# A gated cross-attention block with routed experts: final loads released by a counted quota, a shared unit moved ahead of the expert loop, half of the last additions moved to GpSimd

## What is computed

```python
x = x + tanh(g_xattn) * attention(layernorm(x), ctx, ctx, mask, Wq, Wk, Wv, Wo, 16)
h = layernorm(x)
shared = (silu(h @ Sg.T) * (h @ Su.T)) @ Sd.T
probs = sigmoid(h @ router.T + bias); scores, idx = top_k(probs, 2); scores /= scores.sum(-1)
combined = sum over the two experts e of score_e * ((silu(h @ G[e]) * (h @ U[e])) @ D[e])
x = x + tanh(g_ffn) * (shared + combined)
```

## Time and profile before

| | us |
|---|---|
| median of three timed runs | 181.72 |
| lowest, highest | 181.02, 184.23 |
| the profiled execution's own time | 181.07 |
| its span, first to last instruction | 179.3 |
| busy in the span: TensorE, DVE, ACT, GpSimd | 165.0, 126.9, 109.3, 108.4 |

### The profile page before, as it was taken

One profiled execution on the slowest core, in us unless ns is written; L12 is line 12 of the kernel. 1 busy time (PEld: TensorE's weight loads), 2 busy tenths in 40 slices (PEclk: granted clock), 3 DMA queues, 4 the chain that ended last, 5 costly groups with the idle time before them and its releaser, 6 DMA issues.

```text
span 179.3 us, 4668 instructions
## 1 busy us (share of the span) xinstructions
PE 165.0 (92%) x1424; PEld 140.2 (78%) x1424; DVE 126.9 (71%) x613; ACT 109.3 (61%) x402; POOL 108.4 (60%) x137
## 2 busy tenths in 40 slices
PE   7899889999999999999999999988899999998960
PEld 7777669988889998779998779876586887886840
DVE  2779988756898766798776798778746666663364
ACT  3657997468588267598367698513546666663210
POOL 3666799846796816866706868686444666666200
PEclk9999999999999999999999999999999999999997
DMA  5999994900000000101000000013132222211063
GB/s 154 262 372 375 412 410 191 385 23 4 16 0 18 0 2 4 32 19 44 1 4 0 15 21 32 15 49 91 45 89 65 63 66 78 73 53 35 12 223 117
DMA packets 11095, 17.34 MB, mean 97 GB/s; under 512 B 2075, under 2 KB 6945, under 8 KB 10944
## 3 DMA queue, kind: packets, MB, share of 16 engines
q1 hardware_dynamic: 9504, 14.59, 24.0%
q0 software_dynamic: 1280, 2.20, 3.7%
q10 hardware_dynamic: 288, 0.26, 0.4%
HBM read 9.99 MB, written 7.51 MB: 98 GB/s over the span
## 4 chain that ended last, share of the span: by engine, by line
PE 62%; DVE 13%; ACT 8%; DMA 6%; POOL 5%; issue 4%; SPq 1%
PE misc L397 8%; PE pt L650 7%; PE s_even L360 6%; PE o_bank L386 6%; ACT probs L716 4%; PE pt L371 4%; PE proj_q L317 3%; DMA wq_raw<-wqT 3%; PE proj_k L317 3%; DVE probs L925 3%; PE proj_k L319 2%; PE pt L641 2%; PE proj_k L318 2%; PE proj_q L319 2%; PE proj_q L318 2%
## 5 line engine op out<-in xcount | busy, mean ns | idle before, releaser
L716 ACT ACTIVATE probs<-probs,negmax 128x128 f32<-128x128 f32 x128 | 50.0, 395 | 8.5 <-DVE negmax L925 8.5
L1311 POOL TENSOR_TENSOR probs<-probs,rinv 128x512 f32<-128x512 f32 x32 | 33.1, 1046 | 24.6 <-DVE rinv L939 24.3
L1420 POOL DMA_INDIRECT ys<-probsT,xg x23 | 22.5, 979 | 17.2 <-issue 10.7
L716 ACT ACTIVATION_READ_ACCUMULATOR probs<-probs,negmax 128x1 f32 x128 | 24.4, 191 | 0.0
L925 DVE CUSTOM_DVE_ANT_0 probs<-s_even,mask 128x128 f32<-128x128 f32 x64 | 18.1, 282 | 3.8 <-issue 3.8
L1341 POOL DMA_INDIRECT xs<-xrow,slot x16 | 16.3, 1019 | 6.5 <-issue 3.9
L371 PE MATMUL pt<-ident_sb,probs 128*128 128x128 f32 x128 | 17.6, 277 | 1.6 <-POOL probs L1311 1.1
L360 PE MATMUL s_odd<-kT,qT 64*128 64x128 f32 x128 | 18.5, 285 | 0.0
L360 PE MATMUL s_even<-kT,qT 64*128 64x128 f32 x128 | 18.5, 284 | 0.0
L925 DVE CUSTOM_DVE_ANT_0 probs<-s_odd,mask 128x128 f32<-128x128 f32 x64 | 18.1, 283 | 0.0
L650 PEld LDWEIGHTS pt<-down_sb,v 128*128 128x128 f32 x92 | 12.1, 190 | 7.2 <-issue 7.1
(11 more groups left out here) (279 smaller groups left out, 455.0 us busy)
## 6 DMA issues: line engine op xcount, KB each, us to landing
xs<-pad SPq DMA_DIRECT2D x5, 858.0 KB, 5.8
xg<-xs SPq DMA_DIRECT2D x23, 66.0 KB, 1.9
down_sb<-down SPq DMA_DIRECT2D x1, 1152.0 KB, 8.9
probs<-ys SPq DMA_DIRECT2D x4, 256.0 KB, 4.0
gu_raw<-gu SPq DMA_DIRECT2D x3, 256.0 KB, 6.5
wk_raw<-wkT SPq DMA_DIRECT2D x2, 256.0 KB, 3.8
wq_raw<-wqT SPq DMA_DIRECT2D x2, 256.0 KB, 5.0
mask<-mask SPq DMA_DIRECT2D x8, 64.0 KB, 2.0
```

The costliest lines, as they stand in the source:

```text
L716: e = act.activation(probs[:, r, l, :], probs[:, r, l, :], ACT.Exp, bias=negmax[:, r, l:l + 1], scale=-1.0, accum_out=rowsum[:, r, l:l + 1])
L1311: pool.tensor_tensor(quad, quad, rinv[:, r, 4 * u:4 * u + 4].unsqueeze(2).to_broadcast([P, 4, P]), ALU.mult).then_inc(norm_done, 1)
L1420: pool.indirect_dma_start(out=ys, out_offset=bass.IndirectOffsetOnAxis(ap=xg[n % IN_FLIGHT][:, P:P + 1].bitcast(U32), axis=0), in_=y_sb[n ...
```

## The change

- `FEWEST` = 2 is the least number of blocks with rows on any `y_out` semaphore. DVE's new `quota_steps`, at the end of round 10, make eight integers in two small dependent instructions: 32 or 48, according to whether block 16 + i holds rows.
- SP loads these eight into registers behind its last gather, waits on each `y_out` for the register's value, issues the four loads and its two stores, and only then waits for all 23 scatters.
- Shared unit 0 takes the place of `stay_warm(6)` ahead of the loop, unit 1 takes the place in round 3, and the order behind the loop is pass 2 (with the last block's down inside), pass 3, `down_step(0)`, `down_step(1)`. The silu of unit 0 moves to round 0 on ACT, its product to round 1 on DVE.
- For this the router of the sequences 6 and 7 moves from the banks `proj_q` and `proj_k` to `pt0` and `pt1`, and `down_step(0)` from `pt0` to `proj_k`.
- GpSimd, behind its last scatter, adds the first expert's rows to all four chunks. DVE adds the second expert's, and the shared expert last, after each pair of chunks. The stores wait for that.

```diff
-        shared_banks = [(proj_bank["q"], proj_bank["k"]), (o_bank, misc), (s_bank[0], s_bank[1]), (proj_bank["q"], proj_bank["k"])]
-        d_bank = [pt_bank[0], proj_bank["q"]]
+        shared_banks = [(proj_bank["q"], proj_bank["k"]), (proj_bank["q"], proj_bank["k"]), (o_bank, misc), (s_bank[0], s_bank[1])]
+        d_bank = [proj_bank["k"], proj_bank["q"]]
...
-        route_bank = [misc, misc, proj_bank["q"], proj_bank["q"], proj_bank["k"]]
+        route_bank = [misc, misc, proj_bank["q"], pt_bank[0], pt_bank[1]]
...
-            engine.wait_ge(sum_ready, n + 1)
+            engine.wait_ge(acc_done, 1 + n // 2)
...
+            def quota(i):
+                return sp.value_load(quotas[0:1, i:i + 1], min_val=16 * FEWEST, max_val=16 * (FEWEST + 1))
+
+            sp.wait_ge(quota_ready, 2)
+            due = [quota(i) for i in range(IN_FLIGHT)]
             for i in range(IN_FLIGHT):
-                sp.wait_ge(y_out[i], 16 * len(range(i, BLOCKS, IN_FLIGHT)))
+                sp.wait_ge(y_out[i], due[i])
             for n in range(4):
                 load_y(sp, n)
             store_out(sp, 0)
             store_out(sp, 2)
+            for i in range(IN_FLIGHT):
+                sp.wait_ge(y_out[i], 16 * len(range(i, BLOCKS, IN_FLIGHT)))
...
-            stay_warm(6)
+            pe.wait_ge(counts_read, 1)
+            shared_pass(0, 0)
+            shared_pass(0, 1)
...
                 if n + 2 == EARLY:
-                    pe.wait_ge(counts_read, 2)
-                    shared_pass(0, 0)
-                    shared_pass(0, 1)
+                    pe.wait_ge(h_done, 1)
+                    shared_pass(1, 0)
+                    shared_pass(1, 1)
...
-            shared_pass(1, 0)
+            shared_pass(2, 0)
             block_down(BLOCKS - 1, experts[BLOCKS - 1])
-            shared_pass(1, 1)
-            pe.wait_ge(h_done, 1)
-            shared_pass(2, 0)
             shared_pass(2, 1)
-            down_step(0)
+            pe.wait_ge(hid_ready, BLOCKS)
             shared_pass(3, 0)
             shared_pass(3, 1)
+            down_step(0)
             down_step(1)
...
+            def quota_steps():
+
+                beyond = float(IN_FLIGHT * FEWEST - EARLY) + 0.5
+                dve.tensor_scalar(more[:], iota_sb, beyond, upto[:, CANDIDATES - 1:], ALU.add, ALU.is_le).then_inc(quota_ready, 1)
+                dve.wait_ge(quota_ready, 1)
+                dve.tensor_scalar(quotas[:], more[:], 16.0, 16.0 * FEWEST, ALU.mult, ALU.add).then_inc(quota_ready, 1)
...
+                if n == 1:
+                    hidden(0)
...
+                if n == 2 * EARLY:
+                    quota_steps()
...
-            add_shared(0)
...
+            for half in range(2):
+                for n in (2 * half, 2 * half + 1):
+                    tiles = slice(2 * n, 2 * n + 2)
+                    dve.wait_ge(first_added, n + 1)
+                    dve.tensor_tensor(x_sb[:, tiles, :], y_of[:, tiles, 1, :], x_sb[:, tiles, :], ALU.add).then_inc(second_added, 1)
+                dve.wait_ge(second_added, 2 * half + 2)
+                add_shared(half)
...
+            for n in range(4):
+                tiles = slice(2 * n, 2 * n + 2)
+                pool.wait_ge(in_y[n], 16)
+                pool.tensor_tensor(x_sb[:, tiles, :], y_of[:, tiles, 0, :], x_sb[:, tiles, :], ALU.add).then_inc(first_added, 1)
```

More of the change, by code:

```diff
@@ L40 @@
 IN_FLIGHT = 8
+FEWEST = TOKENS * TOP_K // P // IN_FLIGHT
 EPS = 1e-5
@@ L127, in build @@
         slot = sb("slot", [P, B, TOP_K], U32)
+        more, quotas = sb("more", [P, IN_FLIGHT]), sb("quotas", [P, IN_FLIGHT], I32)
         total, share = sb("total", [P, B]), sb("share", [P, B])
@@ L204, in build @@
         at_ready, counts_read = sem("at_ready"), sem("counts_read")
+        quota_ready = sem("quota_ready")
         table_step, table_ready = sem("table_step"), sem("table_ready")
@@ L209, in build @@
         th_done, hidT_ready, yb_done, y_ready = sem("th_done"), sem("hidT_ready"), sem("yb_done"), sem("y_ready")
-        first_added, sum_ready = sem("first_added"), sem("sum_ready")
+        first_added, second_added = sem("first_added"), sem("second_added")
         xs = nc.dram_tensor("xs", (SLOTS, WIDTH), F32).ap()
@@ L215, in build @@
         y_rows = probs.rearrange("p r l k -> p (r l) k")[:, 0:B * TOP_K, :]
+        y_of = y_rows.rearrange("p (b k) h -> p b k h", k=TOP_K)
         def load_y(engine, n):
@@ L416, in x2_transposes @@
                 if r == LAST:
-                    pe.wait_ge(k_free, PROJ_USES * PAIRS)
+                    pe.wait_ge(pt1_free, GROUPS)
+                elif r == 3:
+                    pe.wait_ge(pt0_free, GROUPS)
                 elif r:
                     pe.wait_ge(at_ready, r)
-                if r == 3:
-                    pe.wait_ge(counts_read, 1)
                 for i, b in enumerate(ROUTED[r]):
@@ L863, in _ @@
                     block_y(n - 1)
+                if n == 0:
+                    silu(0)
                 if n + 2 == EARLY:
-                    silu(0)
+                    silu(1)
             block_y(BLOCKS - 1)
-            for unit in range(1, 4):
+            for unit in range(2, 4):
                 silu(unit)
@@ L1258, in _ @@
                 if n + 1 == EARLY:
-                    hidden(0)
+                    hidden(1)
+                if n == 2 * EARLY:
+                    quota_steps()
             block_hidT(BLOCKS - 1)
-            for unit in range(1, 4):
+            for unit in range(2, 4):
                 hidden(unit)
-            add_shared(0)
[L1264 to L1273, removed]
+            for half in range(2):
[5 more added lines that the diff above has]
+                add_shared(half)
         @block.gpsimd
```

## The result

The changed kernel takes 180.72 us in the median of 20 executions (178.97 to 181.66), the kernel before 181.25 of 20; the ratio is 0.9958 with a 95% interval of 0.9938 to 0.9978. It is faster, by some 0.8 us where 2.2 were forecast, and lies 0.02 above the upper end of the range given (177.6 to 180.7). The profiled execution took 181.44 us with a span of 179.4, itself 0.7 above the median. Medians are of executions at the usual granted clock; one of e12, 187.09 us at a clock of 0.855, is left out.

The account below looks back on a forecast made before the run. TensorE's chain and the result rows' landing were taken to end nearly together, the rows becoming the bound; 2.3 us saved at the additions less 0.15 for stores gave 178.9 us (179.0 for a median), range 177.6 to 180.7.

Parts of the forecast that it names:

- TensorE's tail: Behind the loop: six matmuls (1.4 us) and the 1.41 us idle gap go; down_step(1) ends at 171.25, 3.2 us earlier.
- Ahead of the loop: Six passes of unit 0 replace stay_warm(6) and end at 121.03: cost 0, bounds 0 to 0.3; silu and product 0, at most 0.6.
- The quota steps: Two dependent small DVE steps in a loop round, hidden by nothing: 0.3 us once, bounds 0 and 0.5.
- First load issued 166.16: SP waits for blocks 0 to 20 alone, 3.05 us sooner: first load at 165.86 plus 0.3, landed 169.76.
- The additions: Behind the first landing at 169.8, GpSimd's and DVE's additions with both add_shared end at 174.8 against 177.12: 2.3 us saved.
- The mutual hold-up: GpSimd's and DVE's adds wait for each other except the last 0.18 us; a round of both takes 0.97.
- the rule to the letter: Holder keeps the shared pair for its whole instruction: a GpSimd and DVE round takes 1.15, the sum 0.36 us more.
- The stores: At the end the last two stores go together, not 0.8 apart: 0.15 us taken, at most 0.33.
- the third (loads not early): SP's count still includes the last blocks, so the loads go no earlier: 182.0 us; chance 0.04.
- The fourth (start of the loop): Pass, silu and product of unit 0 hit the loop's start, up to 0.6 + 0.3 on top: 179.8 us; chance 0.09.
- The first: GpSimd and DVE do not hold each other up in the final additions, 0.85 less: 178.1 us; chance 0.20.
- The second: GpSimd takes each next chunk before DVE gets in, so DVE starves, 1.0 more: 180.0 us; chance 0.17 with its kin.

Follow-up runs that it names:

- e12: e10 with down_step(0) in round 22, ahead of the last but one block's down: 178.59 us, ratio to the kernel before 0.9868.
- e4: Changed kernel with only the moved units, banks and new order; waits for all scatters, additions in the old order on DVE: 181.22 us, ratio 0.9997.
- e3: Changed kernel without quota_steps and registers, the counts written as constants for this input (21 blocks), loads still early: 180.04 us, ratio 0.9921.
- e1: Changed kernel with all eight additions on DVE, shared expert still last, GpSimd adding nothing: 180.69 us, ratio 0.9952.
- e5: Changed kernel, but DVE begins its additions only when GpSimd has done all four: 181.91 us, ratio 1.0042.
- e9: Changed kernel with quota_steps in round 3, where DVE idles beside the shared unit, instead of round 10: 179.87 us, ratio 0.9940.
- e10: e9 with all additions on DVE in the earlier order: add_shared(0), chunks 0 and 1, add_shared(1), chunks 2 and 3: 178.72 us, ratio 0.9867.
- e11: e10 with 16 instead of 8 buffers for gathered rows and results, seven registers read: 178.51 us, ratio 0.9846.
- e8: The kernel before with only the early loads, counts as constants for this input (21 blocks): 180.99 us, ratio 0.9997.
- e2: Changed kernel without quota_steps and register waits; SP waits for all 23 scatters by constants: 182.16 us, ratio 1.0047.
- e6: Changed kernel with quota_steps in round 21 instead of round 10: 181.18 us, ratio 1.0012.

## Why the prediction was wrong

- **TensorE's tail: right.** The gap of 1.41 us is gone and the two down_steps follow each other, behind a loop that ended 1.36 late: 172.5 against 171.25 + 1.36 = 172.6. The result rows became the bound, as forecast.
- **Ahead of the loop: right.** The six passes (119.85 to 121.47) end where stay_warm ended, and DVE had no wait for unit 0's product; e4 shows the loop's length unchanged within 0.2 us.
- **The quota steps: mechanism right, size too small.** Forecast 0.3; the profile shows 0.45 at the steps, and e3 says 0.7 for the whole kernel. In the same three profiles (the changed kernel, e1, e5) the scatter of the block just behind the steps took 3.3, 3.7 and 3.2 us to land; in the changed kernel the chain shows what that costs. Whether the steps cause that was not isolated; one of 3.0 stands there in the kernel before too.
- **"First load issued 166.16": the step that failed.** It came at 167.98, 1.82 late. 1.05 of it is the scatter of block 20 starting at 164.94, against 163.59 + 0.3. Of this, 0.61 was lost ahead of the loop's first scatter, 0.45 of it in a stretch that did not change; the rest is the quota steps' excess of 0.15 and the gather that waited for a scatter. Another 0.65 is that scatter's own landing, 2.76 us where its counterpart took 2.1, and 0.1 are SP's waits behind it:

```profile
164.94 2.76 DMA ys<-probsT,xg
```

  The prediction took the landing of one transfer in one execution as fixed. The long one is no accident of this execution either: block 20's scatter landed after 2.5 to 3.2 us in each of the nine profiles with the new order that show it (the changed kernel, e1 to e5, e9, e10, e11), and after 2.1 in both of the old order (the kernel before, e8). Only e12, where `down_step(0)` stands earlier, has the new order and some 2.2. Why, no run isolates. The first landing then came 4.0 us after its issue, not 3.6 (3.6 to 3.9 in the experiments with the new order).
- **The additions: right.** Forecast 4.97 us from the first landing (169.8 to 174.77), measured 4.78. The mutual hold-up, forecast from one row, is shown by e5, and of its sizes the shorter was the better. What I did not ask was what the same work costs on DVE alone: as in e1, the same, and 4.05 in e10's order. The second engine gave nothing, and the new order, with both add_shared behind the landings, cost most: from e9 to e10 the same kernel gains 1.15 us by undoing both (1.3 by the ratios), of which 0.73 is DVE's work behind the landing. The hold-up is the mechanism of the Trainium skill, SBUF — State Buffer, section "Who interferes with whom". These traces agree that one engine is held, but not to the full length of the other's instruction: the two rounds took 1.83 us (172.78 to 174.61), against 1.94 forecast and 2.30 by the rule to the letter.
- **Outside the span: not seen.** The time lies 2.0 us above the span in each of the six kernels with GpSimd's additions (the changed one, e2, e3, e5, e6, e9) (1.94 to 2.10 over their runs) and 1.8 (1.75 to 1.87) in all others, the kernel before among them: 0.2 us that no row of the span holds. The stores, two at a time, landed 0.3 later each, where 0.15 was allowed.

The sum on the profiled execution: 2.15 forecast, less 1.82 for the load, 0.4 for its landing, 0.27 behind DVE's last end (2.6 to the span's end against 2.18 + 0.15), 0.27 outside the span, plus 0.2 for the additions, gives 0.4 slower than the 181.07 of before, which is what it was (181.44). In the medians the gain is 0.5 to 0.8 us. What recurs from profile to profile accounts for most of the distance to the 2.15: 0.4 for the quota, 0.65 for block 20's landing, 0.1 to 0.2 for the first load's, 0.25 for the stores and the end, 0.2 outside the span, less 0.2 for the additions. That is an estimate from the profiles named above, some 1.5 us, and leaves 0.7.

Of the rivals, the third (loads not early) fell: SP did release them two scatters ahead. The fourth (start of the loop) fell with e4. The first fell with e5. The second describes what DVE suffered only in part: it was held up, not starved.

## What to carry to other kernels

Where two branches end together, each half of a change can measure as nothing (e4, e8), and the gain shows only with both. Behind a late landing, leave only what needs it (add_shared(0) goes ahead of it in e10), and do not split it over DVE and GpSimd where both read two operands from SBUF. Put a few small instructions where their engine idles, early enough for the reader behind them.

## What the runs showed of the hardware that was not expected

- A register read on SP, with the register operation and the check of bounds behind it, costs 0.55 us; eight in a row run from 163.0 to 167.5 in e6.
- DVE's 128x256 addition goes from 0.42 to as much as 0.94 us beside GpSimd's, and GpSimd's from 0.72 to 0.90 beside DVE's: both sides are held.
- A 64 KB scatter of GpSimd lands after 2.1 to 2.3 us mostly, and now and then after 3.0 to 4.3, in the kernel before too (up to 3.6). Some of it recurs with the block: block 1's took 3.6 to 4.3 in nine profiles and 2.3 in two. With eight buffers in turn, such a landing can stop TensorE two transfers later.
- The time outside the span was 0.2 us longer whenever GpSimd computed at the end; e1, with the same stores but without GpSimd's additions, has the shorter one. Why, these runs don't tell.
